# A decoder layer with a sorted token mixture: small inputs packed, the fourth weight rounded on another engine, low parts of ctx all on GpSimd

## The reference, cut to what matters

```python
# attention part, b = 4, l = 512, d = 512; _bitlinear rounds x to 8 bits a row and w to {-1, 0, 1} by its mean |w|
i = _bitlinear(x, Wi); f = sigmoid(_bitlinear(x, Wf)); i = silu(i) * (1.0 - f)
h = scan over l of h = f * h + i
g = _bitlinear(x, Wg)
o = _rmsnorm(g) * g_norm_weight * (h * sigmoid(h))
x = _layernorm(x + _bitlinear(o, Wo))
# expert part: tokens 0..24999 and up fall to 4 experts e; Wg = Wu = Wd = ctx
y_e = (silu(x @ ctx[e].T) * (x @ ctx[e].T)) @ ctx[e].T
x = _layernorm(x + y_of_the_token's_expert)
# mixing part: factors (8, 512, 512)
x = _layernorm(x @ factors.sum(0) / sqrt(8) + bias + x)
```

## Time and profile before

| | us |
|---|---|
| median of 3 runs | 393.56 (393.05 to 400.62) |
| profiled execution, its time | 394.12 |
| its span | 392.3 |
| TensorE busy | 289.5 (74%) |
| VectorE busy | 237.5 (61%) |
| ScalarE busy | 231.0 (59%) |
| GpSimd busy | 220.6 (56%) |
| granted TensorE clock, mean | 0.89 |

### The profile page before, as it was taken

How to read it: one execution, slowest core, us unless ns; L and a number is a source line. 1 busy time by engine, 2 the same in 40 slices (tenths; PEclk the granted TensorE clock), 3 DMA queues, 4 the chain that set the end, 5 groups by cost and what they waited for, 6 DMA issues and landing times.

```text
span 392.3 us, 5737 instructions
## 1 busy us (share of the span) xinstructions
PE 289.5 (74%) x1506; PEld 218.3 (56%) x1518; DVE 237.5 (61%) x475; ACT 231.0 (59%) x456; POOL 220.6 (56%) x394
## 2 busy tenths in 40 slices
PE   1476201848438689699899899599579999999960
PEld 0345001525217368487677677487358888888740
DVE  3599698897984685985885685335114444444420
ACT  2779402895945478867786776436325555554431
POOL 3352899787875436646675584653514444444542
PEclk9998855778668899999999999889869999999985
DMA  5999650778873701101300300210221111100000
GB/s 174 390 387 382 142 100 0 158 164 161 162 135 114 155 0 57 54 3 53 109 1 31 118 17 27 102 34 27 82 80 54 56 54 56 54 28 23 27 7 0
DMA packets 17983, 37.03 MB, mean 94 GB/s; under 512 B 1951, under 2 KB 2207, under 8 KB 17952
## 3 DMA queue, kind: packets, MB, share of 16 engines
q0 software_dynamic: 6496, 15.74, 17.2%
q1 hardware_dynamic: 11456, 20.92, 16.2%
HBM read 26.68 MB, written 10.76 MB: 95 GB/s over the span
## 4 chain that ended last, share of the span: by engine, by line
PE 35%; POOL 6%; issue 5%; DMA 5%; ACT 3%; DVE 3%; POOLq 0%; ACTq 0%; DVEq 0%; SPq 0%
PE bank_m L1275 4%; PE bank_m L1276 4%; PE bank_m L1279 4%; PE bank_z L1275 3%; PE bank_z L1276 3%; PE bank_z L1279 3%; PE bank_y L1275 3%; DMA sorted_rows<-r,place 3%; PE bank_y L1279 3%; PE bank_y L1276 3%; DMA rows<-sorted_rows 2%; PE bank_tr L1246 2%; POOL n_d L330 2%; PE bank_q L1246 2%; POOL x L370 1%
## 5 line engine op out<-in xcount | busy, mean ns | idle before, releaser
L329 POOL TENSOR_SCALAR n_v<-n_dev 128x1 f32<-128x1 f32 (+1 forms) x46 | 10.1, 219 | 66.6 <-ACT x L636 29.6
L1275 PE MATMUL bank_y<-c_hi,h_hi 128*128 x76 | 32.7, 431 | 2.6 <-ACT h_hi L604 1.6
L904 DVE TENSOR_TENSOR act_z<-bank_z,act_z 128x512 f32<-128x512 f32 x19 | 13.1, 691 | 35.3 <-ACT act_z L618 35.3
L1275 PE MATMUL bank_m<-f_hi,m_hi 128*128 128x512 f32 x76 | 32.1, 422 | 3.2 <-DVE f_lo L885 2.4
L1275 PE MATMUL bank_z<-c_hi,a_hi 128*128 x76 | 32.9, 432 | 1.8 <-ACT a_hi L604 1.8
L375 POOL DMA_INDIRECT out<-r,token_of x19 | 20.6, 1087 | 23.1 <-ACT r L643 18.6
L1276 PE MATMUL bank_z<-c_lo,a_hi 128*128 x76 | 31.5, 415 | 0.0
L1276 PE MATMUL bank_y<-c_lo,h_hi 128*128 x76 | 30.7, 404 | 0.0
L1276 PE MATMUL bank_m<-f_lo,m_hi 128*128 128x512 f32 x76 | 30.6, 403 | 0.0
L330 POOL TENSOR_TENSOR n_d<-n_v,minus_half 128x1 f32<-128x1 f32 (+1 forms) x46 | 28.2, 614 | 3.9
L370 POOL TENSOR_TENSOR x<-x,bias_b 128x512 f32<-128x512 f32 x19 | 24.9, 1313 | 8.7 <-PE bank_q L1246 8.4
(11 more groups left out here) (208 smaller groups left out, 907.2 us busy)
## 6 DMA issues: line engine op xcount, KB each, us to landing
...
sorted_rows<-pad_row SPq DMA_DIRECT2D x1, 1539.0 KB, 17.1
...
w_stage<-in_wi_t SPq DMA_DIRECT2D x1, 1024.0 KB, 10.8
...
```

The costliest lines, as they stand in the source:

```text
L904: v.tensor_tensor(act_z[:], bank_z[:], act_z[:], ALU.mult).then_inc(s.hid, 1)
L1275: t.matmul(bank[:], hi[:, c, :], w_hi(c), start=(c == 0), stop=False)
```

## The change

Five small inputs (tokens, row numbers, slot constants, identity, triangle) become one array `small` of 375 columns, loaded in one transfer, with views in place of the five tensors. x group 1 is loaded right behind group 0, ahead of the weights, and its squares, maxima, scale, rounding and transposes go to earlier places of turn 0. w_o's sum goes from behind `forget(0, 1)` to the place of `square_x(1)`; its total from turn 1 to turn 0; its rounding goes to VectorE. `find_slots` and `next_fills` go ahead of `gate_i(0, 0)`. GpSimd makes all 16 low parts of ctx, four of them at the start of turn 1, and `high_of_ctx` runs one group of four earlier. The wait for the pad transfer stands ahead of `weight_ready(W_O)`.

```diff
...
-                sp.dma_start(tokens[:], tok).then_inc(s.token_in, 16)
-                sp.dma_start(before[:], before_in).then_inc(s.before_in, 16)
+                sp.dma_start(small[:], small_in).then_inc(s.small_in, 16)
                 load_x(0)
-                sp.dma_start(ident[:], ident_in).then_inc(s.ident_in, 16)
+                load_x(1)
                 load_weights(W_F)
                 load_weights(W_I)
-                sp.dma_start(consts[:], slot_in).then_inc(s.consts_in, 16)
                 load_weights(W_G)
-                load_x(1)
                 load_weights(W_O)
...
GpSimd
                 power_x(0)
+                power_x(1)
                 fill_events()
...
-                power_x(1)
                 weight_ready(W_G)
                 places()
                 scale_g(0)
-                low_of_ctx(range(0, 2))
                 power_x(2)
                 add_factor(1)
 
                 for turn in range(1, MERGE + 1):
                     g, p = turn, turn - 1
                     if turn == 1:
-                        round_weights(W_O)
+                        low_of_ctx(range(0, KC))
+                        pool.wait_ge(s.padded, 16)
                         weight_ready(W_O)
-                        pool.wait_ge(s.padded, 16)
-                        pool.wait_ge(s.numbers_in, 16)
                     else:
                         power_1(p - 1)
+                        low_of_ctx(range(4 * turn - 1, 4 * turn))
                         add_factor(2 * turn - 1)
                     scale_o(p)
                     if turn > 1:
                         scatter_rows(p - 1)
                     scale_g(g)
                     add_factor(2 * turn)
-                    low_of_ctx(range(3 * turn - 1, 3 * turn + 2))
                     power_x(g + 2)
+                    low_of_ctx(range(4 * turn, 4 * turn + 3 + turn // MERGE))
                     number_rows(p)
...
ScalarE
-                square_x(0, 0)
-                square_x(0, 1)
+                for g in range(2):
+                    square_x(g, 0)
+                    square_x(g, 1)
                 weight_sum(W_F)
...
-                square_x(1, 0)
-                square_x(1, 1)
+                weight_sum(W_O)
                 weight_ready(W_G)
...
                     forget(g, 1)
+                    if turn == 1:
+                        weight_ready(W_O)
...
                     if turn == 1:
-                        weight_ready(W_O)
+                        high_of_ctx(1, range(KC))
...
-                    high_of_ctx(turn, range(KC))
+                    if turn < MERGE:
+                        high_of_ctx(turn + 1, range(KC))
...
VectorE
                 quantise_x(0)
+                max_x(1, 0)
+                max_x(1, 1)
+                scale_x(1)
                 weight_scale(W_F)
...
-                scale_x(1)
-                quantise_x(1)
                 weigh_eps()
+                find_slots()
+                next_fills()
                 gate_i(0, 0)
...
                     max_o(p, 1)
+                    if turn == 1:
+                        weight_scale(W_O)
+                        round_weights(W_O)
+                        slot_offsets()
                     scale_x(g + 1)
                     quantise_x(g + 1)
...
-                    if turn == 2:
-                        low_of_ctx(range(N_POOL_LOW, N_POOL_LOW + 1))
-                    if turn == MERGE:
-                        low_of_ctx(range(N_POOL_LOW + 1, N_EXPERTS * KC))
                     residual_1(p)
...
TensorE
                 project_f(0)
+                transpose_x(1)
                 weight_total(W_G)
                 project_i(0)
+                weight_total(W_O)
                 project_g(0)
-                pe.wait_ge(s.xqt, 1)
-                transpose_x(1)
                 spread_max(1)
...
```

More of the change, by code:

```diff
@@ L40 @@
 TAIL = 2 * N_GROUPS - LEAD + 2
-N_POOL_LOW = 11
 def by_name(names, make):
@@ L63, in low_half, with split_columns, decoder_layer @@
     return v[:, 0:v.shape[1]:2]
+def split_columns(tile, widths, types):
+    ends = [sum(widths[:i + 1]) for i in range(len(widths))]
+    return [tile[:, e - w:e].bitcast(d) if d is not I32 else tile[:, e - w:e] for e, w, d in zip(ends, widths, types)]
 def scattered_group(n):
     return min((n + 3) // 2, N_GROUPS - 1) if n < SURE else N_GROUPS - 1
-def decoder_layer(nc, x, tok, ctx_t, wf_t, wi_t, wg_t, wo_t, g_weight, factors, bias, ident_in, before_in,
-                  number_in, slot_in, out):
+def decoder_layer(nc, x, small_in, ctx_t, wf_t, wi_t, wg_t, wo_t, g_weight, factors, bias, out):
     sorted_rows = nc.dram_tensor("sorted_rows", [N_SLOTS * P, ROW], F32, kind="Internal").ap()
@@ L99, in decoder_layer @@
         bias_b = sb("bias_b", [P, D])
-        ident = sb("ident", [P, P])
+        small = sb("small", [P, 2 * N_TILES + N_SLOTS + N_EVENTS + 2 * P], I32)
         ident_h = sb("ident_h", [P, P], F16)
@@ L105, in decoder_layer @@
         place = sb("place", [P, N_TILES], I32)
-        numbers = sb("numbers", [P, N_TILES], I32)
+        tokens, numbers, consts, ident, before = split_columns(
+            small, (N_TILES, N_TILES, N_SLOTS + N_EVENTS, P, P), (I32, I32, F32, F32, F32))
         xq = sb("xq", [P, GT, D])
@@ L133, in decoder_layer @@
             w_stage = sb("w_stage", [P, 4, KC * D], F32, early)
-            before = sb("before", [P, P], F32, early)
             ones = sb("ones", [P, P], F32, early)
-            tokens = sb("tokens", [P, N_TILES], I32, early)
-            consts = sb("consts", [P, N_SLOTS + N_EVENTS], F32, early)
             pad_row = sb("pad_row", [P, ROW], F32, early)
@@ L392, in number_slots @@
                     link(pool.tensor_tensor(number[:], order[:], gain[:], ALU.subtract), s.route)
-                    pool.wait_ge(s.ident_in, 16)
-                    pool.wait_ge(s.consts_in, 16)
+                    pool.wait_ge(s.small_in, 16)
                     pool.tensor_tensor(diagonal[:, 0, :], number[:].rearrange("p t e -> p (t e)"), ident[:, 0:N_EVENTS],
@@ L665, in _ @@
                 forget(0, 1)
-                weight_sum(W_O)
                 square_g(0, 0)
@@ L925, in residual_3 @@
                     v.tensor_scalar(n3_mean[:, i], n3_sum[:, i], -1.0 / D, None, ALU.mult).then_inc(s.mean3, 1)
-                def low_of_ctx(chunks):
-                    for c in chunks:
-                        dve.wait_ge(s.hi, c + 1)
-                        v.tensor_tensor(c_lo[:, c, :], c_stage[:, c, :], c_hi[:, c, :].bitcast(F32), ALU.subtract
-                                        ).then_inc(s.split_dve, 1)
                 def weight_scale(m):
@@ L953, in choose @@
                 def choose():
-                    dve.wait_ge(s.token_in, 16)
+                    dve.wait_ge(s.small_in, 16)
                     for e in range(1, N_EXPERTS):
@@ L1008, in _ @@
                 rescale_f(0, 0)
-                max_x(1, 0)
-                max_x(1, 1)
+                quantise_x(1)
                 rescale_f(0, 1)
@@ L1025, in _ @@
                 weigh_g(0, 1)
-                find_slots()
-                next_fills()
                 max_x(2, 0)
@@ L1036, in _ @@
                     output(p, 1)
-                    if turn == 1:
-                        weight_scale(W_O)
-                        slot_offsets()
                     rescale_i(g, 0)
@@ L1138, in ranks_in_tiles @@
                     pe.wait_ge(s.chosen, 1)
-                    pe.wait_ge(s.before_in, 16)
+                    pe.wait_ge(s.small_in, 16)
                     pe.wait_ge(s.ones, 1)
@@ L1289, in up @@
                     if n == 0:
-                        pe.wait_ge(s.split, N_POOL_LOW)
-                        pe.wait_ge(s.split_dve, N_EXPERTS * KC - N_POOL_LOW)
+                        pe.wait_ge(s.split, N_EXPERTS * KC)
                         pe.wait_ge(s.slot_off, 1)
@@ L1324, in _ @@
                     if turn == 1:
-                        weight_total(W_O)
                         spread_slots()
```

25 lines of the change are left out of this document (7 added, 18 removed).

## The result

The changed kernel takes 380.83 us (median of 4 runs, 379.39 to 384.98) against 393.5 us for the kernel before (4 runs beside it). The ratio is 0.970, with a 95% interval of 0.960 to 0.980: **faster by 3.0%, or 12.7 us by the medians**. I come back to that, since half of what follows is read from it.

The account below looks back on a forecast made before the run. Turn 1's stall of about 16 us, from w_o's rounding on GpSimd, was taken as the bound. Turn 1's 11.8 us plus 0.4 in turns 2 and 3 gave 12.2 off 393.56: 381.4 us, range 375 to 385.

Parts of the forecast that it names:

- What bounds the kernel: Turn 1: a stall of about 16 us, with VectorE standing still behind GpSimd and TensorE and ScalarE waiting.
- part 1's cause: Turn 1: w_o's rounding on GpSimd causes the stall; moving it removes 14.9 us there, adds 2.5 on VectorE.
- The later path wins: Turn 1: of VectorE's path and the pad fill, the fill ends later and sets quantise_o(0) at 55.4, saving 11.8 us.
- the fill lands at 51: Turn 1: the pad-row fill of sorted_rows, sharing DMA with accumulate 1, lands at 51 us instead of 46.1.
- I am wrong if the fill lands by 47: Turn 1: the prediction's own test, failed if the pad fill lands by 47 us or after 53.
- VectorE's path, 51.9: Turn 1: VectorE, rounding w_o from 44.3 to about 47 us, reaches quantise_o(0) at about 51.9, a gain of 15.3.
- the fill isn't delayed, VectorE is the bound: Rival, chance 0.15, turn 1: gain 15.3 us plus 0.4 to 3.3, giving 375.0 to 377.9 us.
- Part 2, the start: Kernel start: x group 1 goes ahead of three weights; W_f comes up to 1.4 us later, 1.0 taken, hidden by the fill.
- Part 3, turns 2 and 3: Turns 2 and 3: VectorE loses five subtractions; 0.4 us saved of 3.2 and 6, bounds 3.3 saved to 1.5 lost.
- GpSimd becomes the pace of turns 2 and 3: Rival, chance 0.18: subtractions ahead of scale_o and late accumulates cost up to 1.5 us, fill at 52: 384.3 us.
- the row of 3.87 us: Earlier trace: VectorE's c_lo subtraction, 0.68 us when quiet, took up to 3.87 beside GpSimd's, read as waiting out their row.
- some 2 us: Turn 1: by the skill's lock rule, VectorE waits for one subtraction only and w_o is rounded some 2 us sooner.

Follow-up runs that it names:

- a_pad_behind: Changed kernel with the wait for the pad transfer moved from ahead of the fourth weight's last half to turn 2, ahead of scatter_rows(0): 380.69 us.
- a_acc1_behind: Changed kernel with accumulate 1 issued behind GpSimd's four subtractions and the wait for the pad transfer in turn 1: 381.30 us.
- b_wo_vector: Kernel before with one edit, the fourth weight w_o rounded by VectorE behind max_o in turn 1: 385.09 us.
- a_spread: Changed kernel; GpSimd subtracts four ctx chunks at the end of turns 1 to 3, VectorE the last four; pad wait in turn 2: 379.49 us.
- a_factor_shift: Changed kernel with accumulates 6 and 7 one place later each, 6 behind token_of_row(0), 7 behind token_of_row(1) in turn 4: 380.17 us.
- a_late_factors: Changed kernel with accumulate 6 moved to turn 4 behind token_of_row(1), accumulate 7 to the end of turn 4: 390.30 us.
- a_low_vector: Changed kernel with the last five of 16 ctx subtractions back on VectorE, one in turn 2 and four in turn 3: 383.78 us.
- a_clo_behind: Changed kernel with GpSimd's four subtractions of ctx 0 moved behind scale_o(0) in turn 1: 385.78 us.

## Why the prediction was right, and where it wasn't

Forecast 381.4, measured 380.8: 12.2 us against 12.7. The sum is right, but its terms are off in opposite directions: turn 1 gave 14.4 us for the forecast's 11.8, and what lies between it and `residual_1(4)` lost 1.2 us where 0.4 saved was forecast. That these cancel is luck.

- **What bounds the kernel, and part 1's cause.** Right, and shown: moving the two instructions alone gives 12.7 us at `quantise_o(0)`. One reading of the earlier trace rows is off: VectorE's instructions don't all end where GpSimd's do. `x_q` ended at 52.42, while GpSimd's first one ran until 54.98; only the last `xq` ended with GpSimd's second (62.50 and 62.22).
- **"The later path wins": the fill lands at 51.** This step failed. It landed at 44.6, and a_pad_behind shows that its wait is covered. The forecast priced the fill by the loads of `rows`, which take 7.2 us under an accumulate. But those are issued into an accumulate that already runs; the fill was issued 11 us ahead of accumulate 1, and there the late one pays: accumulate 1 took 12.2 us to land in the changed kernel, against 8.9 in the kernel before and 9.1 in a_acc1_behind. The fill took 18.4 us without the accumulate in a_acc1_behind, inside the 17.4 to 19.8 with it. "I am wrong if the fill lands by 47" was the right test, and it says wrong.
- **VectorE's path, 51.9.** Right as a mechanism: the rounding is what both engines came from, and `quantise_o(0)` started at 52.78. But GpSimd's chain behind the weight ended with VectorE's (52.75 and 52.70), because `o_v` to `o_q` took 4.1 us (48.63 to 52.75) for the forecast's 3.1. The forecast let the rounding start at 44.3, when the subtractions end; they ended at 45.1 and it ended at 47.4 (forecast 47). So the rival "the fill isn't delayed, VectorE is the bound" is what happened in turn 1, with 14.4 us for its 15.3.
- **Part 2, the start.** 1.0 us was taken; W_f's sum started 0.18 us later (11.37 against 11.19). x1 filled the hole in the DMA (its share from 5 to 7 us is 0.85, 0.39 before), the lower bound. Unseen was what else these moves do: `places` 7 us earlier, and with it `w_q` not behind GpSimd's own list, and accumulate 1 at 38.6 instead of 46 us. Without them (b_wo_vector) turn 1 loses 1.7 us and turns 2 and 3 more.
- **Part 3, turns 2 and 3: 0.4 saved.** Mis-sized, by one term. From `quantise_o(0)` to `up(0)` 0.8 us was to be lost, and 2.3 were. Counted from `quantise_o(0)`, the forecast has accumulates 3, 4 and 5 at 13.0, 22.2 and 31.4 us; measured 12.7, 22.1 and 33.1. The first two are right. But the forecast let the next accumulate go 9.2 us after the one before, and 5 left 10.9 us after 4, which took 10.7 us to land. Those 1.7 us are all that turns 2 and 3 lost beyond the forecast. In the forecast's frame `up(0)` starts at 119.56 - 11.8 = 107.8, and it started at 106.6. That this is within 1.2 us is the same luck as above: 2.6 us sooner in turn 1, 1.5 lost behind. It isn't a limit that holds `up(0)` whatever turn 1 does: in a_spread `up(0)` (102.71) keeps 2.1 of the 2.7 us that `quantise_o(0)` gained. a_factor_shift and a_late_factors do show what accumulate 6 beside the load of `rows(0)` covers: 4.4 and 3.8 us at `up(0)`. Where the 1.0 us between `quantise_o(0)` and `(1)` is lost is open. Without the five moved subtractions (a_low_vector) the way to `residual_1(4)` is 1.9 us longer, so moving them was worth more than 0.4.
- **The rival "GpSimd becomes the pace of turns 2 and 3"** has its traces, 1.19 us at `quantise_o(2)`. But a_spread, with no subtraction ahead of `scale_o` in any turn, has `quantise_o(1)` and `(2)` no closer together (18.2 and 20.1 us for 18.0 and 19.9), and neither has a_low_vector, which thins turn 3 alone. What GpSimd waits for ahead of `scale_o(2)` is `f_sum`.

On the lock, the row of 3.87 us was the better guide for this order than the rule of the Trainium skill, "SBUF — State Buffer", section "SBUF: two separate sides", by which the loser would wait for one instruction. In the changed kernel and the five others with the same order there, VectorE's pass ended 1.09 to 1.10 us after the last of GpSimd's four, with 3.36 to 5.43 us for 1.29; with the row elsewhere (a_clo_behind, a_spread) it took 1.29. But a_acc1_behind sides with the rule: beside the same row it took 2.41 us and got in between two subtractions, and the weight was rounded 2.4 us sooner behind W_f's sum, the "some 2 us" of the prediction. In all six executions that held the pass to the end, and in the row of 3.87, an accumulate is issued directly ahead of the row, and the subtractions are recorded at 1.8 us each, 1.2 apart, so that they overlap; without that issue they are recorded one behind the other, at 1.3 to 1.7 us, or 2.2 where one waited for VectorE. When in the row the pass came made no difference: 1.1 to 3.2 us behind its start in the six, 2.4 in a_acc1_behind. So it is the place behind the DMA issue that goes with the long hold-up. Why it does, no run shows.
